# Two interleaved threads of a four-layer kernel: another table of step times

## The reference, cut to what matters

```python
x = L0_attn_x
for l in 0, 1, 2, 3:
    xn = layernorm(x)
    s = attn_l(xn, ...)
    g = silu(ffn_l(xn, ...))
    x = x + s * g
```

## Time and profile before

| what | value |
|---|---|
| median of three runs | 3852.59 us (3845.99 to 3853.17) |
| the profiled execution's own time | 3852.74 us |
| its span | 3851.0 us |
| mean granted clock of TensorE | 0.878 |
| PE busy | 3115.1 us, 81% |
| VectorE busy | 2426.6 us, 63% |
| ACT busy | 1662.7 us, 43% |
| POOL busy | 596.6 us, 15% |
| DMA | 355.91 MB, mean 92 GB/s |
| most costly group of the page | POOL L1404, 434.7 us in 320 |

### The profile page before, as it was taken

One profiled execution on the slowest core, in us unless ns is written; L12 is line 12 of the kernel. 1 busy time (PEld: TensorE's weight loads), 2 busy tenths in 40 slices (PEclk: granted clock), 3 DMA queues, 4 the chain that ended last, 5 costly groups with the idle time before them and its releaser, 6 DMA issues.

```text
span 3851.0 us, 43741 instructions
## 1 busy us (share of the span) xinstructions
PE 3115.1 (81%) x16174; PEld 1567.3 (41%) x16174; DVE 2426.6 (63%) x4576; ACT 1662.7 (43%) x2458; POOL 596.6 (15%) x425
## 2 busy tenths in 40 slices
PE   3647868997699868997699968998699977996698
PEld 1124423553245433554245532554235532464145
DVE  4634876568756776568765776668755786634442
ACT  3504625465255634465154644446154643432231
POOL 2001000311023010321013010321013110211030
PEclk8568969998799979998699989998799988997696
DMA  3151175302842165402843047412753128412261
GB/s 112 27 95 58 46 123 139 113 14 77 145 144 68 28 106 154 124 22 60 152 133 88 20 104 121 151 39 50 136 133 102 32 81 136 137 58 65 57 203 45
DMA packets 331910, 355.91 MB, mean 92 GB/s; under 512 B 98529, under 2 KB 264225, under 8 KB 330081
## 3 DMA queue, kind: packets, MB, share of 16 engines
q1 hardware_dynamic: 331697, 353.11, 39.1%
HBM read 302.74 MB, written 49.66 MB: 92 GB/s over the span
## 4 chain that ended last, share of the span: by engine, by line
PE 52%; DVE 28%; DMA 7%; ACT 5%; issue 4%; POOL 2%; SPq 2%; ACTq 0%; DVEq 0%; POOLq 0%
DVE MX L1596 7%; PE PS L1805 6%; PE PS L1828 6%; PE PS L1832 5%; PE PS L1659 5%; PE PS L1667 5%; PE PS L1103 3%; DVE U L891 3%; PE PS L1773 3%; DVE U L898 3%; DMA UU<-k_scratch 3%; PE PS L1784 2%; DVE D L1650 2%; POOL D L1404 1%; DVE D L948 1%
## 5 line engine op out<-in xcount | busy, mean ns | idle before, releaser
L1404 POOL TENSOR_TENSOR D<-D,GW 128x512 f32<-128x512 f32 x320 | 434.7, 1359 | 1409.1 <-ACT D L1477 1173.6
L783 ACT ACTIVATE U<-U 128x2048 f32<-128x2048 f32 x256 | 488.0, 1909 | 184.3 <-DVE U L891 99.4
L1645 DVE SCALAR_TENSOR_TENSOR D<-D,PS 128x512 f32<-128x512 f32 x336 | 229.2, 682 | 399.2 <-ACT D L1481 283.6
L1477 ACT ACTIVATE D<-PS 128x512 f32<-128x512 f32 x336 | 200.2, 596 | 610.2 <-PE PS L1828 610.2
L1805 PEld LDWEIGHTS PS<-WST,D 128*128 128x128 f32 (+1 forms) x2688 | 353.0, 198 | 163.4 <-DVE D L1650 96.0
L1805 PE MATMUL PS<-WST,D 128*128 128x128 f32 (+1 forms) x2688 | 380.3, 286 | 29.3 <-DVE D L1650 29.2
L1832 PE MATMUL PS<-XT,WST 128*128 128x512 f32 (+1 forms) x672 | 372.6, 637 | 29.2 <-DVE D L1645 28.0
L898 DVE SCALAR_TENSOR_TENSOR U<-PP,RD,QB 128x512 f32<-128x512 f32 x512 | 364.1, 780 | 47.5 <-ACT QB L780 28.8
L1103 PE MATMUL PS<-U,resident 128*32 128x512 f32 x2048 | 304.6, 675 | 102.3 <-ACT U L783 102.3
L1828 PE MATMUL PS<-XT,WST 128*128 128x512 f32 (+1 forms) x672 | 369.6, 633 | 7.7 <-DMA WST<-in_pairs_dram 4.7
L1596 DVE TENSOR_REDUCE MX<-PS 128x2 f32<-128x1024 f32 x256 | 298.4, 1221 | 84.9 <-PE PS L1751 84.9
(11 more groups left out here) (345 smaller groups left out, 3907.2 us busy)
## 6 DMA issues: line engine op xcount, KB each, us to landing
GW<-gates_scratch SPq DMA_DIRECT2D x320, 256.0 KB, 4.3
WST<-in_pairs_dram SPq DMA_DIRECT2D x336, 192.0 KB, 2.4
U<-band_scratch SPq DMA_DIRECT2D x32, 1280.0 KB, 14.6
UU<-in_w_dram SPq DMA_DIRECT2D x64, 512.0 KB, 7.6
UU<-pad_scratch SPq DMA_DIRECT2D x8, 1792.0 KB
UU<-q_scratch SPq DMA_DIRECT2D x24, 384.0 KB
UU<-k_scratch SPq DMA_DIRECT2D x24, 384.0 KB
e_scratch<-D SPq DMA_DIRECT2D x8, 1024.0 KB, 4.5
```

The source lines that it names most:

```text
L783: e.activation(ring(i), ring(i), ACT.Gelu).then_inc(S["act"], 1)
L1404: e.tensor_tensor(AV[:, n % 3, :], AV[:, n % 3, :], GW[:, p // 2 % GWS, p % 2, :], ALU.mult).then_inc(S["gated"], 1)
```

## The change

Only the numbers of the table are new: `TURN` and the ten tuples of `STARTS`. They were computed with a rule that the table before didn't have: an engine stays free for a short while where a step of the more urgent thread will be ready sooner than the other thread's step would take. No step, instruction, wait, buffer or size is changed. `TURN` goes from 428.30 to 425.80.

Counted over all steps of the run, each time that a step of one thread now stands on the other side of a step of the other one: 1778 on PE, 1277 on VectorE, 707 on ACT, 49 on SyncE, 18 on POOL. In most of them a step of A comes later in relation to B's.

The diff, cut to some lines of the tables. A line holds 16 steps; the line that begins with 183.43, for one, is steps 48 to 63 of A on PE before.

```diff
-TURN = 428.30
+TURN = 425.80
...
     "a_act": (
...
-        173.80, 191.06, 194.65, 213.26, 214.21, 215.15, 216.10, 216.60, 262.23, 284.64, 285.66, 287.61, 288.42, 289.37, 292.92, 293.86,
...
+        167.93, 190.96, 194.05, 206.36, 207.30, 208.24, 209.18, 209.67, 256.84, 278.11, 278.61, 279.93, 280.83, 281.77, 284.82, 285.96,
...
     "a_pe": (
...
-        69.68, 71.58, 73.47, 78.26, 83.00, 87.78, 92.52, 97.32, 102.06, 105.87, 107.77, 108.72, 109.66, 111.84, 115.71, 121.87,
-        126.60, 129.67, 133.44, 139.54, 144.83, 147.14, 150.05, 156.38, 160.19, 164.00, 166.85, 170.66, 178.57, 183.31, 183.31, 183.37,
-        183.43, 183.48, 184.87, 186.76, 198.58, 211.15, 212.10, 213.05, 214.00, 214.94, 245.40, 250.45, 255.75, 261.07, 263.30, 274.38,
-        283.47, 286.31, 291.76, 292.71, 295.31, 296.50, 299.36, 300.55, 303.15, 311.30, 311.44, 311.86, 313.76, 314.05, 314.41, 314.59,
...
+        180.55, 184.82, 186.52, 188.33, 197.30, 202.40, 205.21, 206.15, 207.09, 208.03, 240.37, 243.91, 246.85, 255.72, 257.91, 267.89,
...
     "a_sp": (
-        -64.99, 194.30, 199.03, 213.93, 216.90, 219.88, 222.86, 230.96, 236.26, 241.56, 246.86, 263.68, 293.20, 295.65, 297.45, 303.49,
-        307.14, 357.17,
+        -71.52, 194.96, 199.48, 207.02, 209.84, 212.66, 215.47, 222.93, 227.91, 232.88, 241.73, 258.43, 285.62, 288.44, 290.24, 293.30,
+        297.69, 348.12,
     ),
...
     "b_pe": (
...
-        152.55, 152.55, 153.51, 154.46, 155.41, 155.41, 157.33, 158.28, 159.22, 159.22, 161.14, 162.09, 163.04, 163.04, 164.95, 165.90,
-        166.85, 167.80, 168.77, 169.71, 170.66, 171.61, 172.58, 173.53, 174.47, 174.47, 175.44, 176.39, 182.36, 192.18, 194.80, 219.79,
-        220.31, 221.78, 222.94, 224.10, 225.25, 226.41, 227.57, 228.72, 229.88, 231.04, 232.20, 233.35, 234.51, 235.67, 236.82, 237.98,
...
+        142.66, 142.66, 143.58, 144.49, 145.43, 145.43, 146.65, 147.56, 148.50, 148.50, 150.33, 151.24, 152.18, 152.18, 153.11, 154.93,
+        155.87, 155.87, 156.86, 158.68, 159.62, 159.62, 160.54, 161.45, 163.30, 163.30, 164.23, 165.13, 167.10, 179.33, 181.12, 208.97,
+        209.46, 210.94, 212.10, 213.26, 214.42, 215.58, 216.74, 217.89, 219.05, 220.21, 221.37, 222.53, 223.69, 224.85, 226.01, 227.17,
...
     "b_sp": (
-        20.31, 20.31, 20.64, 20.98, 21.31, 21.64, 107.98, 141.57, 143.17, 152.76, 155.62, 159.43, 163.25, 167.06, 170.87, 174.68,
-        177.55, 183.52, 187.18, 201.69, 204.14, 205.94, 261.32, 263.09, 267.72, 318.68, 319.11, 319.55, 319.99, 320.43, 320.87, 321.30,
...
+        11.99, 11.99, 12.33, 12.66, 12.99, 13.33, 97.72, 132.48, 134.09, 142.87, 145.64, 148.71, 152.39, 156.08, 159.83, 162.60,
+        166.28, 168.25, 172.76, 188.55, 191.36, 193.16, 249.41, 251.17, 253.57, 307.90, 308.33, 308.77, 309.20, 309.64, 310.07, 310.51,
...
```

More of the change, by code:

```diff
@@ L171, in laid_out @@
     return dict(x=w("L0_attn_x"), consts=packed(CONSTS + MASKS), resident=packed(RESIDENT), passing=packed(PASSING), last=packed(LAST), pairs=wst.reshape(PAIRS, P, 3 * P), w1=w1)
-TURN = 428.30
+TURN = 425.80
 STARTS = {
     "a_act": (
[8 rows of a table removed]
[8 rows of a table added]
     ),
     "a_dve": (
[9 rows of a table removed]
[9 rows of a table added]
     ),
     "a_pe": (
[11 rows of a table removed]
[11 rows of a table added]
     ),
     "a_pool": (
-        1.68, 20.45, 281.18,
+        2.04, 12.10, 274.67,
     ),
     "a_sp": (
-        -64.99, 194.30, 199.03, 213.93, 216.90, 219.88, 222.86, 230.96, 236.26, 241.56, 246.86, 263.68, 293.20, 295.65, 297.45, 303.49,
-        307.14, 357.17,
+        -71.52, 194.96, 199.48, 207.02, 209.84, 212.66, 215.47, 222.93, 227.91, 232.88, 241.73, 258.43, 285.62, 288.44, 290.24, 293.30,
+        297.69, 348.12,
     ),
     "b_act": (
[13 rows of a table removed]
[13 rows of a table added]
     ),
     "b_dve": (
[14 rows of a table removed]
[14 rows of a table added]
     ),
     "b_pe": (
[23 rows of a table removed]
[23 rows of a table added]
     ),
     "b_pool": (
[3 rows of a table removed]
[3 rows of a table added]
     ),
     "b_sp": (
[6 rows of a table removed]
[6 rows of a table added]
     ),
```

## The result

The changed kernel takes 3942.11 us in the median of four runs (3936.42 to 3945.55), against 3852.88 (3845.99 to 3854.46) of the kernel before beside it: ratio 1.0234, 95% interval 1.0215 to 1.0252. The prediction was 3940. The profiled execution has a span of 3943.8 us, 92.8 more than before.

A forecast was written before the change was run, and what follows sets the result against it. Bound: the chain of waits (52% TensorE, 28% VectorE, neither alone), with thread B's delays lengthening the turn. 11.5+0.7−1.5+1.8 = +12.5 us a mixed turn, times 7 = 87.5, on 3852.7: 3940 us; range 3866 to 3968.

The forecast's parts named there:

- (a): SyncE, layer 3: A's store behind B's stack loads delays L1751; +11.5 us a turn (T: issue of B's q loads).
- the store's part on those comes after what is queued: On about 13 of 16 DMA engines, A's store waits behind B's stack loads, landing 2.5 us after them.
- R1: Rival: DMA engines share instead of queueing, L1751 7 us later; +8.0 us a turn, 3909 us; chance 0.15.
- R2: Rival: A's store isn't held and the new table gains; −4.8 us a turn, 3819 us; chance 0.11.
- R3: Rival: no stall of the store, give-backs in full; +2.1 us a turn, 3867 us; chance 0.08.
- (b): Tail of layer 2's pairs and update: 2.7 us sooner, then +2.7 and +0.7 given back; together +0.7 us a turn.
- (c): Ahead of layer 3's exponentials: L1154 and L1162 move into their loop; −1.5 us before it, +1.8 in it.
- (d): Turn start: A's L1074 steps go behind B's where PE is full; 0 us, at most 3.8.
- (e): The rest: L1103, pads and other steps moved a little in full or covered stretches; 0 us, bounds −1 and +1.

The follow-up runs named there:

- sp_swap: The kernel before with only A's score store and skewed loads moved behind B's stack stores and loads on SyncE; ratio 1.0253.
- act_both: The changed kernel with A's score store and skewed loads issued by ACT's queue instead of SyncE's; ratio 1.0124.
- k_by_act_after: The changed kernel with B's three layer-3 k loads issued by ACT's queue instead of SyncE's; ratio 1.0188.
- second_half2: The kernel before with nearly the whole second half of the turn in the changed kernel's order; ratio 1.0036.
- den_late: The kernel before with A's L1154 and L1162 (and ACT's step 56) at the changed kernel's places, L1168 not moved; ratio 1.0107.
- transposes_late: The changed kernel with A's four transposes L1143 on TensorE moved behind B's score matmuls; ratio 1.0195.
- sp_back: The changed kernel with A's score store and skewed loads put back ahead of B's stack stores on SyncE; ratio 1.0228.

## Why the prediction was right

**(a), the stall: right, step by step.** Forecast and chip: store issued T+5.6 and T+5.6; landed T+20.5 and T+20.7; L1143 at T+26.6 and T+26.8; L1751 at T+29.5 and T+30.7. Of the 1.2 us missing at the end, 0.8 are in L1143, which took 3.68 us and not 2.87, since TensorE's clock was low in the 14.09 us of waiting before it; 0.2 were there before it and 0.2 lie between it and L1751:

```profile
2344.00:2356.00 12.00, 2.07 (x8) 1.78 (x8) 7.09 (x42) 0.00 (x0) 0.00 (x0) 0.50 0.88 193
```

PEclk is 0.50 there, the lower level of 1.2 GHz, after which the 16 transposes run as slowly as in turn 0. `sp_swap` shows the place in SyncE's queue as the cause, and the packets show how: three quarters of the store stand behind the stack loads. The forecast's step "the store's part on those comes after what is queued" is right, and the band store that it was read from does the same: 512 of its packets start at T+10.2 to T+11.8, then none until T+15.8. R1's mechanism was seen from another queue: there the store took 10.9 us (`act_both`), where R1 had 4.5+5.8 = 10.3. R1 fails because the transfers of one queue don't share in this way.

**The rule that one ring is worked off in order** (the Trainium skill, "DMA: Bandwidth & Descriptors", section "Queues, rings and completion order") has the changed kernel's 15.1 us and its 5 us without a packet of the store with it. The same section says that an engine takes turns between the queue rows that it has work for; the 292 and 293 packets in `k_by_act_after` and the 10.9 us in `act_both`, neither 4.5 nor 15.1, agree with that.

**R2 and R3 are out**: the store didn't land at T+10.

**(b), the tail of layer 2's pairs: the gain right, the give-back mis-sized.** −2.9 for −2.7, then +1.1 for +3.4. L1617 to L1293 took 8.4 us before and takes 10.8 now, +2.4 as against 2.7; the split is 0.6 longer, as forecast. What I missed is between L1293 and the split's L1042, 6.2 before and 4.5 now. There A's transposes L1111 now keep TensorE busy ahead of L1293, and B's projections L1733 run at a higher granted clock, 0.96 (2327 to 2331) for 0.53 (2281 to 2285) (ns, min/median/max; first the changed kernel's, then the kernel before's):

```profile
L1733 PE MATMUL PS<-XT,resident x4: 592/592/697, 2327.5 to 2328.9; 128*128 128x512 f32 x4
```

```profile
L1733 PE MATMUL PS<-XT,resident x4: 904/1057/1220, 2281.5 to 2284.2; 128*128 128x512 f32 x4
```

**(c): the gain right, the price mis-sized by half.** −1.9 for −1.5, +3.6 for +1.8. I had let 2.75 us of idle TensorE take up part of the moved 4.57. They don't. The moved work was smaller, 1.94 us for L1154 and 1.95 for L1162 (3.49 at its old place), and a little of A's L1222 and L1223 left the loop; but what came in was paid in full: the whole loop of the changed kernel has 56.58 us of work in 61.0 where the kernel before has 53.65 in 57.6. 2.9 us more work, 3.4 more time, the idle rest stayed (4.4 for 4.0).

```profile
2411.30:2472.30 61.00, 56.58 (x312) 19.60 (x318) 25.37 (x68) 41.36 (x79) 1.01 (x1) 0.96 0.42 92
```

```profile
2356.70:2414.30 57.60, 53.65 (x295) 18.37 (x294) 28.26 (x74) 40.27 (x78) 1.01 (x1) 1.00 0.45 94
```

**(d): right.** The ffn piece has 84.80 us of TensorE in 85.30, as before; its length doesn't change.

**(e): wrong by 1.7 us.** I had put the moved steps 73 to 94 at nothing; `second_half2` shows 2.1 us for them and their kin without any stall. Which of them it is stays open. The 1.3 us that the maxima won (L1751 to L1762, 39.1 for 40.4) I had also put at nothing; they seem to come with the later places of L1154, since `den_late`, which moves little else, has 39.4 there without the stall.

The errors have both signs (−0.2, −2.3, +1.4, −1.3, −0.4, +1.8, +1.7) and nearly cancel. That the sum is out by 0.7 us a turn owes something to luck; that its large term is the stall does not.

## What to carry to other kernels

When a table or a planner reorders queues, follow each transfer that moves behind another, and ask what is ahead of it in the DMA engines when it is issued, not only whether its issuer is free: here a landing of 4.5 us became one of 15.1, and 10.9 from another queue. Then look for the first instruction in an in-order queue that waits for it with the other thread's work behind. And don't expect that taking one such wait away gives its time back: the late store reached TensorE again as a late band load (`transposes_late`), and the late softmax as a late stack store (`sp_back`). Idle slivers in a loop that two engines hand back and forth, here 4.0 us of 57.6, were no room for more work.

## What the runs showed of the hardware that I had not expected

- A store of 1024 KB that lands in 4.5 us on an idle queue took 15.1 behind six loads of its own queue, and 10.9 from ACT's queue beside the same loads.
- On one queue the order held packet by packet: 128 of the store's 512 packets started at once, the other 384 only when the stack loads were nearly done, in all seven turns. Between two queues the packets alternated, 292 to 293 in 3 us.
- The three k loads let L1751 start 12.5 us after the end of their issue, with the q loads right ahead of them and with 4.6 us between; 8.4 and 8.5 of it are their own 1,152 packets.
- TensorE's clock in short idle times decides several microseconds a turn, both ways: 0.8 us of loss in L1143 (granted clock 0.50 before it), 1.7 us of gain ahead of the split (L1733's median 592 ns for 1057, granted clock 0.96 for 0.53).
